# Value rows copied side by side through DRAM, expert weights turned in the setup, and the last quarters' routing moved, in a two-layer gated cross-attention kernel

## What is computed

```python
x = x + tanh(g_xattn[0]) * L0_xattn(layernorm(x), ctx)   # q from x, k and v from ctx, softmax over 77 keys, wo
x = x + tanh(g_ffn[0])   * L0_ffn(layernorm(x))          # 8 experts, top 2 by a router softmax
#   h = x @ w1[e].T ; y = h[256:] * silu(h[:256]) ; out = sum over the two e of weight_e * (y @ w2[e].T)
x = x + tanh(g_xattn[1]) * L1_xattn(layernorm(x), ctx, mask)
x = x + tanh(g_ffn[1])   * L1_ffn(layernorm(x))          # token shift, sigmoid gate, squared relu
```

## Time and profile before

| | |
|---|---|
| median of 3 runs | 378.57 us (378.55 to 381.73) |
| the profiled execution | 381.57 us, its span 379.8 us |
| busy | PE 301.1 us, PEld 212.8, DVE 267.3, ACT 204.3, POOL 212.2 |
| chain that ended last, by engine | DVE 31%, PE 28%, issue 12%, POOL 8%, ACT 8%, another core or an unknown queue 3% |
| mean granted TensorE clock | 0.865 of full speed |
| DMA packets | 27,189, 24.97 MB |

### The profile page before, as it was taken

One profiled execution on the slowest core, in us unless ns is written; L12 is line 12 of the kernel. 1 busy time (PEld: TensorE's weight loads), 2 busy tenths in 40 slices (PEclk: granted clock), 3 DMA queues, 4 the chain that ended last, 5 costly groups with the idle time before them and its releaser, 6 DMA issues.

```text
span 379.8 us, 7644 instructions
## 1 busy us (share of the span) xinstructions
PE 301.1 (79%) x2230; PEld 212.8 (56%) x2230; DVE 267.3 (70%) x747; ACT 204.3 (54%) x534; POOL 212.2 (56%) x398
## 2 busy tenths in 40 slices
PE   3995999787797778478899948759878987696874
PEld 3673655555465458466678737536545554454653
DVE  0464899989997966453454416668979899698574
ACT  3633788566663633323455514347666767486622
POOL 7238665554786746472000165655676876986381
PEclk9998799899896995666999988966898889698789
DMA  4880991000000002111232233210000000000012
GB/s 113 229 215 28 437 413 59 0 2 3 15 30 14 30 28 76 37 56 29 77 84 73 83 91 84 63 37 14 16 14 16 22 22 2 0 2 3 2 37 74
DMA packets 27189, 24.97 MB, mean 66 GB/s; under 512 B 5316, under 2 KB 25485, under 8 KB 26637
## 3 DMA queue, kind: packets, MB, share of 16 engines
q1 hardware_dynamic: 25101, 20.28, 16.6%
q0 software_dynamic: 2048, 4.20, 3.9%
HBM read 9.92 MB, written 14.55 MB: 64 GB/s over the span
## 4 chain that ended last, share of the span: by engine, by line
DVE 31%; PE 28%; issue 12%; POOL 8%; ACT 8%; another core or an unknown queue 3%; DMA 0%; SPq 0%; POOLq 0%; DVEq 0%; ACTq 0%
DVE pr L469 8%; DVE mx L441 7%; DVE smm L486 5%; PE scores_ps L1446 5%; ACT pr L422 4%; PE bank L1428 3%; PE bank L294 2%; PE bank L1429 2%; PE bank L1430 2%; PE bank L1437 2%; PE scores_ps L356 2%; DVE xrn L1042 1%; POOL rstd L107 1%; PE scores_ps L1412 1%
## 5 line engine op out<-in xcount | busy, mean ns | idle before, releaser
L422 ACT ACTIVATE pr<-pr 128x512 f32<-128x512 f32 (+1 forms) x96 | 51.9, 551 | 22.6 <-DVE pr L469 22.3
L1530 POOL DMA_INDIRECT back<-expert_rows,row_of x32 | 31.4, 980 | 57.6 <-DMA expert_rows<-w_sb 42.9
L294 PE MATMUL bank<-ident,pr 128*128 128x128 f32 x320 | 59.9, 317 | 0.5
L383 ACT COPY pT<-bank 128x512 f32<-128x512 f32 (+1 forms) x96 | 47.7, 516 | 13.3 <-PE bank L294 10.4
L356 PE MATMUL scores_ps<-kbd,work 32*128 32x308 f32 x256 | 38.8, 530 | 16.7 <-DVE pr L469 15.8
L441 DVE TENSOR_REDUCE mx<-scores_ps 128x8 f32<-128x616 f32 x64 | 47.7, 787 | 5.3 <-PE scores_ps L356 5.3
L469 DVE TENSOR_TENSOR pr<-scores_ps,mx 128x512 f32<-128x512 f32 (+1 forms) x96 | 48.8, 564 | 0.1
L294 PEld LDWEIGHTS bank<-ident,pr 128*128 128x128 f32 x320 | 44.9, 165 | 6.2 <-ACT work L413 4.3
L1479 DVE TENSOR_TENSOR w_sb<-w_sb,bank 128x256 f32<-128x256 f32 x39 | 16.4, 420 | 38.3 <-ACT w_sb L1458 29.0
L486 DVE TENSOR_REDUCE smm<-pr 128x16 f32<-128x1024 f32 x32 | 39.0, 1218 | 4.5 <-ACT pr L422 4.5
L343 PE MATMUL bank<-pT,vbd 128*32 128x128 f32 x768 | 39.2, 308 | 1.6 <-ACT pT L383 1.6
(11 more groups left out here) (241 smaller groups left out, 656.4 us busy)
## 6 DMA issues: line engine op xcount, KB each, us to landing
expert_rows<-back SPq DMA_DIRECT2D x4, 2048.0 KB, 13.7
w_sb<-expert_rows SPq DMA_DIRECT2D x39, 64.0 KB
expert_rows<-w_sb SPq DMA_DIRECT2D x39, 64.0 KB
w_sb<-in_L_ffn_w_dram SPq DMA_DIRECT2D x4, 512.0 KB, 6.1
xs<-in_x_dram SPq DMA_DIRECT2D x4, 256.0 KB, 3.8
w_sb<-in_L_ffn_w_dram SPq DMA_DIRECT2D x4, 256.0 KB, 6.7
out_dram<-xs SPq DMA_DIRECT2D x3, 256.0 KB, 2.3
expert_rows<-xrn,row_of POOLq DMA_INDIRECT x32
```

Of the source, the lines that this page charges most:

```text
L294: mm = pe.transpose(ps[:, c0 + P * i:c0 + P * i + P], pr[:, u, P * c:P * c + P], ident[:])
L383: act.copy(pT[:, 4 * P * n:4 * P * n + P * len(chunks)], ps[:, c0:c0 + P * len(chunks)]).then_inc(pT_ready, 1)
L422: act.activation(part, part, ACT.Exp, scale=SCALE).then_inc(exp_done, 1)
L1530: pool.indirect_dma_start(back[:, b, k, :], None, xrow, bass.IndirectOffsetOnAxis(ap=row_of[:, b, k:k + 1], axis=0)).then_inc(gathered[b % ...
```

## The change

1. **Values once.** `yrep`, its zeroing and its copies are gone, and so is the zeroing of `pr`. `values(p)` multiplies yT of two batches by wv, 77 rows each, eight pairs instead of sixteen batches; the result goes to `v_rows`, a view of 77 partitions of `back`. `keep_values` writes these rows to a DRAM tensor, `spread_values` reads them back side by side into `vc`, in two pieces: batches 0 to 3 in the setup, batches 4 to 15 at the head of SP's next block, before the clears. `build_values` of layer 0 waits for the piece it needs: piece 0 for tiles 0 to 3, piece 1 from tile 4 on. The 13 rest keys now stand without gaps (104 partitions instead of 128).
2. **The clears** take their zeros from half of `xrn`, zeroed in the setup, in 17 transfers of up to 512 KB instead of 5; the zeroing of `back` in slot 0 is gone. `normalise` of quarter 2 waits for the clears.
3. **Expert weights turned in the setup**, two groups after each pair of values from pair 2 on, in three banks; VectorE copies w2 instead of ScalarE. Each pair of experts has its own semaphore. SP's order is: pairs 0 and 1, keep piece 0, pair 2, spread piece 0, pair 3.
4. **Routing.** Quarter 2 is done earlier in slots 16 and 17 (`transpose_rows` and `positions` ahead of the output matmul, `columns` on ScalarE, `top_two` and `first_table` ahead of `oT` in slot 17, `rows` after it, scatter (8, 0) before the last deviations). Quarter 3 is done in the experts' slots -1 to 2, the second table in slots 3 to 6, its words in slot 8, and `weights(0)`, `weights(1)` in slots 9 and 10.

```diff
+        SPREADS = ((0, 4), (4, B))
+        def keep_values(sp, n):
+            lo, hi = SPREADS[n]
+            sp.dma_start(v_dram[:, lo:hi, :], v_rows[:, lo:hi, :]).then_inc(v_kept, 16)
+        def spread_values(sp, n):
+            lo, hi = SPREADS[n]
+            sp.wait_ge(v_kept, 16 * (n + 1))
+            for region, (k0, k1, copies) in enumerate(((0, KM, P // KM), (KM, S2, H // 2))):
+                rows = v_dram[k0:k1, lo:hi, :].rearrange("k b c -> k (b c)")
+                sp.dma_start(vc[0:copies * (k1 - k0), region, lo:hi].rearrange("p b l d -> p (b l d)"),
+                             rows.unsqueeze(0).to_broadcast([copies, k1 - k0, (hi - lo) * 2 * D])
+                             ).then_inc(v_spread, 16)
...
             def build_values(pool, g, u):
+                if layer == 0:
+                    n = sum(1 for lo, _ in SPREADS if lo <= 2 * g + u)
+                    pool.wait_ge(v_spread, 2 * 16 * n)
...
+                    expert_weights(0)
+                    expert_weights(1)
+                    sp.wait_ge(v_copied_act, 1)
+                    sp.wait_ge(v_copied_dve, 1)
+                    keep_values(sp, 0)
+                    expert_weights(2)
+                    spread_values(sp, 0)
+                    expert_weights(3)
...
             def sync(sp):
-                sp.wait_ge(zero_ready, 1)
+                keep_values(sp, 1)
+                spread_values(sp, 1)
                 flat = xrow.rearrange("(p r) d -> p (r d)", p=P)
...
                 def between(pe, s):
-                    if s == -1:
+                    if s == 0:
+                        Tensor.transpose_rows(pe, NQ - 1)
+                    if s == 1:
+                        Tensor.logits(pe, NQ - 1)
+                    if s == 2:
+                        Tensor.positions(pe, NQ - 1)
+                    if s == 3:
                         Tensor.count(pe, 1)
-                    if s == 4:
+                    if s == 7:
                         Tensor.pack(pe, 1)
```

More of the change, by code:

```diff
@@ L88, in flamingo_kernel @@
         w2_sb = sb("w2_sb", [P, E, I])
-        w_loaded = sem("w_loaded")
+        v_kept = sem("v_kept")
+        v_spread = sem("v_spread")
+        SPREADS = ((0, 4), (4, B))
+        xrn = sb("xrn", [P, B, D])
+        back = sb("back", [P, B, 2, D])
+        v_rows = back[0:S2].rearrange("p b k d -> p b (k d)")
+        v_dram = nc.dram_tensor("value_rows", [S2, B, 2 * D], F32, kind="Internal").ap()
+        def keep_values(sp, n):
[9 more added lines that the diff above has]
+                             ).then_inc(v_spread, 16)
         x_loaded = [sem(f"x_loaded{q}") for q in range(NQ)]
@@ L523, in flamingo_kernel @@
             bv_bc = rx[:, 0, :]
+            w_loaded = [sem(f"w_loaded{i}", su) for i in range(E // 2)]
+            wT_done = sem("wT_done", su)
+            wT_high = sem("wT_high", su)
+            wT_low = sem("wT_low", su)
             y_loaded = sem("y_loaded", su)
@@ L629, in _, with values, expert_weights @@
                 def _(pe):
-                    def values(b):
-                        if b >= 2:
-                            pe.wait_ge(v_copied_dve if b % 2 else v_copied_act, b // 2)
-                        for part in range(2):
-                            mm = pe.matmul(pbank(b % 2)[:, 256 * part:256 * part + 256], yrep[:, b, part, :],
-                                           wv01[:], start=True, stop=True)
-                        mm.then_inc(v_done, 1)
+                    def values(p):
+                        if p >= 2:
+                            pe.wait_ge(v_copied_dve if p % 2 else v_copied_act, p // 2)
+                        for i in range(2):
+                            mm = pe.matmul(pbank(p % 2)[0:S2, 256 * i:256 * i + 256], yT[:, 2 * p + i, :], wv01[:],
+                                           start=True, stop=True)
+                        mm.then_inc(v_done, 1)
+                    def expert_weights(n):
+                        pair, g = n // 3, n % 3
+                        pe.wait_ge(w_loaded[pair], 32)
+                        if n >= 3:
+                            pe.wait_ge(wT_low, n - 2)
+                        else:
+                            pe.wait_ge(k_copied, 6)
+                        for i in range(4):
+                            part = (w1_sb[:, 2 * pair + g, i, :] if g < 2 else
+                                    w2_sb[:, 2 * pair + i // 2, P * (i % 2):P * (i % 2) + P])
+                            mm = pe.transpose(pbank(5 + n % 3)[:, P * i:P * i + P], part, ident[:])
+                        mm.then_inc(wT_done, 1)
                     pe.wait_ge(ident_ready, 1)
@@ L809, in flamingo_kernel @@
         packed = sb("packed", [1, 2, WORDS], I32)
-        back = sb("back", [P, B, 2, D])
         FIRST_ROWS, SECOND_ROWS = 11, 28
@@ L862, in packed_ps @@
                 return spare(2, 0, WORDS) if h == 0 else spare(3, 0, WORDS)
-            zeros = back[:].rearrange("p b k d -> p (b k d)")
-            ZC = 2 * B * D
+            zeros = xrn[:].rearrange("p b d -> p (b d)")[:, ZC:2 * ZC]
             per_row = REGION * D
@@ L1208, in after_shift @@
                         Vector.normalise(dve, (t - 7) // 4)
+                    if t == B + 1:
+                        Vector.top_two(dve, QH)
+                        Vector.first_table(dve)
                 def after_slot(dve, t):
@@ L1250, in exponential, with columns @@
                     act.activation(ex[:, tiles, :], ex[:, tiles, :], ACT.Exp).then_inc(ex_ready, 1)
+                def columns(act, q):
+                    act.wait_ge(xT_done, q + 1)
+                    act.wait_ge(lg_done, q)
+                    act.copy(xrT[:], spare(3, 0, 4 * P)).then_inc(xT_read, 1)
                 def after_slot(act, t):
```

315 lines of the change are left out of this document (133 added, 182 removed).

## The result

| | before | after |
|---|---|---|
| median of 4 runs beside each other, us | 379.27 | 411.87 |
| all four, us | 378.55 to 381.73 | 409.60 to 417.37 |
| profiled execution: time / span, us | 381.57 / 379.8 | 417.37 / 415.6 |
| mean granted clock of TensorE | 0.865 | 0.827 |

The changed kernel is slower: the ratio is 1.085, 95% interval 1.080 to 1.090. The medians differ by 32.6 us, the two profiled executions by 35.8 us (the one of after is the longest of its four). The prediction was worked out from the profiled execution, so its steps are held against the 35.8; about 3 us of that are the one long execution and belong to no known step.

A forecast was written before the change was run, and what follows sets the result against it. VectorE bounds layer 0's attention; at the border to the experts, the chain through quarter 3's routing. 12.9 - 1.1 + 21.0 - 1.2 - 12.3 = +19.3 on the median of 378.57 gives 397.9, so 398 us; range 386 to 412.

The forecast's parts named there:

- setup: Start to tile 0: pair 3 queues behind the first spread's 12.1 us, tile 0 at 45.0 instead of 32.09; +12.9 us.
- slots 0 to 3: First attention slots: the 3.51 us zeroing of `back` goes, of which VectorE had waited 1.09 us; -1.1 us.
- second spread: Slot 4: piece 1 lands at 88.5, POOL waits 22.4 us for it, VectorE loses 21.0; +21.0 us.
- slots 4 to `xrn` of quarter 3: Later attention slots: `weights` leaves slots 11 and 15 (-1.2), `xrn` moves from 146.79 to 144.2; -3.5 us together.
- `xrn` to `row_of`: Routing of quarter 3: positions at 154.6 instead of 155.21, `row_of` at 155.5; -2.3 us.
- `row_of` to block 9: Scatters end at 165.4 against 170.4, second table covered, load 9 done at 170.5 against 182.79; -7.6 us.
- block 9 to the end of the experts: Experts' blocks from block 9 on: no change forecast, the sum ended at load 9; 0 us.
- after the experts: From the experts' end to the kernel's end: no change forecast; 0 us.
- Number of engines: Spread transfers: outermost length sets the DMA engines, so main keys run on 2, rest keys on 8, the keep on 11.
- Rate of one engine: Spread transfers: 26.1 GB/s for each DMA engine, from the clears' 401 GB/s; bounds 18.4 and 30.2.
- rival of 16 engines: Spreads: all 16 engines carry them, deciding from some 8 engines on for the main keys; -11.6, 367 us; chance 0.12.
- The clears: 17 clears behind the second spread take 21 us, to 110, needed no earlier than 113: hidden, 3 us to spare.

The follow-up runs named there:

- e3: The changed kernel with the main keys' broadcast cut into four transfers by tiles in both pieces, still 2 copies outermost: 396.12 us, ratio 1.094 to before.
- e1: The changed kernel with each copy of the value rows as its own transfer (2 main keys, 8 rest keys), both pieces: 371.39 us, ratio 1.021 to before.
- e4: e1 with copies sent straight from the SBUF rows, without the keep in DRAM: 367.57 us, ratio 1.008 to before.
- f6: The changed kernel with only the main keys copy by copy, rest keys still one broadcast of 8 copies: 384.00 us, ratio 1.006 to before.
- f7: f6 with the setup's spread of piece 0 issued behind pair 3 of the experts' weights: 381.22 us, ratio 1.002 to before.
- f8: The changed kernel with values computed in all copies as before, without transfers: 385.69 us, ratio 1.014 to before.
- g1: f7 again, unchanged, as base for g2 and g3: 361.32 us, ratio 0.999 to before.
- g3: g1 with the whole second table earlier (parts in experts' slots 3, 3, 4, 5, words in slot 5): 358.96 us, ratio 0.987 to before.
- f5: The kernel before, unchanged, traced on a chip of the slower sort: 379.11 us.
- h1: The kernel before, unchanged, traced once more, on a chip of the faster sort: 365.55 us.
- g2: g1 with the second half's packed words (matmul and copy) in experts' slot 6 instead of 7 and 8: 358.88 us, ratio 0.992 to before.
- section 1: Follow-up on the number of engines, four variants of the changed kernel's spreads (copy by copy, cut by tiles, from SBUF): ratios 1.008 to 1.094 to before.

## Why the prediction was right, and where its sizes were wrong

The direction, the mechanism and both waits were right; 398 us was 14 us too low, and 411.87 lies at the very edge of the range of 386 to 412. That it lies inside is in part luck, since all eight steps came out above the forecast. By steps, profiled execution against profiled execution (the last column is the stretch before and after):

| step | forecast | measured | |
|---|---|---|---|
| setup | +12.9 | +16.3 | 32.09 to 48.34 |
| slots 0 to 3 | -1.1 | +0.3 | 22.20 to 22.53 |
| second spread | +21.0 | +21.8 on VectorE | POOL waits 24.1 |
| slots 4 to `xrn` of quarter 3 | -3.5 | 0.0 | 92.24 to 89.96, of which 2.3 is POOL's slack |
| `xrn` to `row_of` | -2.3 | -0.2 | 13.63 to 13.44 |
| `row_of` to block 9 | -7.6 | -5.7 | 22.63 to 16.89 |
| block 9 to the end of the experts | 0 | +2.9 | 65.98 to 68.85 |
| after the experts | 0 | +0.4 | 131.0 to 131.5 |
| sum (rounded) | +19.3 | +35.8 | 379.8 to 415.6 |

- **Number of engines: right.** The 28 missing packets told it; the rows at 0.12 to 0.13, e3 and the packet counts of after and of e1 to e4 and f6, each met exactly, show it. The rule of the Trainium skill that I named then holds here.
- **Rate of one engine, 26.1 GB/s: right.** 946 KB in 40.17 us less 2.1 of start-up is 24.9 GB/s; the spread took 40.2 us where 38.4 were forecast, and the keep 5.7 where 5.4 were. Counted from tile 0, the spread landed 3.1 us later than forecast (0.6 of it between the keep's landing and the spread's start) and POOL asked for it 1.4 us later: hence a wait of 24.1 instead of 22.4. POOL's slack was 2.3 us, not 1.4, so VectorE lost 21.8, near the 21.0.
- **Setup, too low by 3.3.** The failed sentence is "the keep has landed by 24 too and the spread stands queued behind pair 2". The keep did land by 24, but SP issued the spread only then, at 23.84, when pair 2 was almost through, and the spread's own start-up of some 2.1 us followed; the DMA engines idled (share 0.13 at 24 to 26). The remaining 1.4 us is the rate: 315 KB from 25.9 to 40.05 is 22.3 GB/s. The rows are shorter (4 KB) and pair 3 runs beside them; which of the two slows the engine isn't shown.
- **Slots behind the stall, too low by 3.5.** The forecast let the slots go on at their old pace. From slot 4 to slot 7 before takes 15.7 us (54.29 to 70.00), after 15.1 and POOL's slack of 2.3 (94.96 to 110.05): 1.7 us more, with the clock at 0.50 up to 99 and 0.77 up to 104.5; e3, with the same stall, 1.9 more. I had priced the stall and not this tail. The other 1.8 us can't be put down to the stall. Kernels without one gained over this stretch, against before on the same sort of chip, 3.3 us (f6), 4.0 (f7), 1.6 (f8), 2.1, 1.7 and 2.3 (g1 to g3); the forecast of 3.5 is at the upper end of these.
- **Slots 0 to 3, too low by 1.4.** The 1.1 us for the zeroing of `back` can't be seen: after takes 22.5 us there, before 22.2, 22.8 and 22.7 in its three traces (before, f5, h1). Why stays open.
- **Ahead of `row_of`, too low by 2.1.** I had the case as a bound ("such a wait ahead of `row_of`, in full") and took a mean instead. The wait came, 4.5 us (before had one of 4.0 there, at 155.34). On chips without such waits this step went from 10.5 us in h1 (148.50 to 159.01) to 9.1 in g1 (148.86 to 157.92), 8.8 in g2 and 8.7 in g3: -1.4 to -1.8, less than the forecast of -2.3.
- **Block 9 and behind it, too low by 4.8.** "The second table in slots 3 to 6 ends before the scatters do, so it is covered" fails in this trace: `block_row_i` was ready at 212.41, while the last scatter was issued at 207.64 and, by 0.96 + 1.8 us as forecast, landed at 210.4. But VectorE, which makes the table, had just stood 2.3 us in a wait of the kind above, until 210.18. In e1 to e4, g1 and g2, with the table in the same slots and no such wait, it was ready before the last scatter was even issued (g1: 164.86 and 167.22); in f6 to f8, which have these waits, it came 4.9 us behind that issue. So the cover was right for a chip without these waits, and the failed part is again their price. Behind block 9, the sum ended at load 9, while PE's first product of block 9 needs `packed`, which nobody had been named to wait for: blocks 9 to 12 took 7.1 us in after and 5.5 in before. That is 1.6 of the 2.9 us; 1.5 more lie behind the last block's transpose (8.5 to 10.0 us), unexplained.
- **The rival of 16 engines** (367 us, 3% below before) was wrong in size. With the engines all at work e1 was 2% above and f7 level with before, because everything behind the start of tile 0 was worth 4.4 us in place of 14.6 (h1: 363.8 - 32.45 = 331.4; g1: 361.1 - 34.16 = 326.9) and because copies one by one fill half of the bandwidth (section 1). "Some 8 engines on for the main keys" wasn't tried; for the rest keys 8 are enough (f6).
- **The clears** held nothing: the DMA engines are idle from 117 on, the first scatter is issued at 139.51 and quarter 2 is normalised at 166.21.
- **A slip in the sums:** halfway between 398 and 418 is 408, not 407; nothing hangs on it.

## What to carry to other kernels

Write down the outermost length of both sides of every new transfer before its bytes: 2 copies outermost are two engines, and all that is queued behind waits for these two. Then look at the other end, for a transfer that is split by copies to gain engines loses partitions, and the best form may mix both. And when work moves to an earlier place, follow each of its results to the engine that reads it: a gain ends where the first unmoved or more deeply queued result (here a copy of four numbers behind another load) is needed.

## What the runs showed of the hardware that I had not expected

- A narrow transfer throttles what is queued behind it on the free engines too: SP needed 47.5 us to issue the 17 clears behind the second spread and 10.5 for one load of pair 3, and the DMA share fell to 0.12 in stretches while fourteen engines were free. The clears ran at full rate only from 94 on, and on the two engines ended 10 us later than elsewhere.
- With all engines busy, 64 destination partitions take 200 to 213 GB/s, against 405 to 414 for the clears from 128; 13 partitions take 83 GB/s at a share of 0.78 (e1, e4).
- A stall of the whole core costs more than its length: 1.7 us in the three slots behind it in after and 1.9 in e3, with the clock at 0.50 right behind the stall.
- The same program differs by 15 us between chips (f5 and h1). The slower traces have waits of up to 5.4 us for an event that the profile calls remote, all from quarter 3's routing to the end of the experts and none in the rest; the faster ones have none.
- The packets of a queue count its engines: the data's runs, and one more packet for each engine that a transfer uses, met the pages of before, after and six further kernels exactly (e1 to e4, f6 and f8; 27,741 in e1).
